# A gated cross-attention and feed-forward block on one core: the layer-normed rows of batches 1 to 3 brought in features first, with means and deviations spread through memory, in place of transpositions on TensorE

## The reference, cut to what matters

```python
x = x + tanh(g_xattn[0]) * xattn(layernorm(x), k_cache=ctx, v_cache=ctx, wq, wk, wv, wo)
x = x + tanh(g_ffn[0])   * ffn(layernorm(x), up, down, up_scale, down_scale, output_scale)

def xattn(x, ...):          # x: (4, 512, 512), ctx: (4, 512, 512)
    q, k_new, v_new = x @ wq.T, x @ wk.T, x @ wv.T
    k, v = concat([ctx, k_new], 1), concat([ctx, v_new], 1)
    return softmax(q @ k.T / sqrt(512)) @ v @ wo.T

def ffn(x, ...):            # hidden 2048, both weights only by their sign
    return relu((x @ sign(up).T) * up_scale) @ sign(down).T * down_scale * output_scale

def layernorm(x):           # no gain and no bias
    return (x - mean(x)) / sqrt(var(x) + 1e-5)
```

## Time and profile before

| What | Value |
|---|---|
| Median of 3 runs | 628.89 us (628.64 to 629.04) |
| The profiled execution's own time | 627.86 us |
| Its span in the trace | 625.8 us |
| Mean granted TensorE clock | 0.999 of full speed |
| PE busy | 617.2 us, 99% of the span |
| DVE, ACT, POOL busy | 247.1, 177.6, 73.9 us |
| Moved by DMA | 30.07 MB, 48 GB/s on average |

### The profile page before, as it was taken

The page is one execution under the profiler, slowest core; times in us unless marked ns, Lnnn a source line. Parts: engine busy times, 40 slices in busy tenths (PEclk is TensorE's granted clock), DMA queues, the critical chain, the costliest instruction groups (busy, mean ns, idle before and its releaser), DMA issues.

```text
span 625.8 us, 6852 instructions
## 1 busy us (share of the span) xinstructions
PE 617.2 (99%) x2898; PEld 513.2 (82%) x2898; DVE 247.1 (39%) x429; ACT 177.6 (28%) x273; POOL 73.9 (12%) x52
## 2 busy tenths in 40 slices
PE   7999999999999999999999999999999999999997
PEld 6888888888888888888888888888888888888885
DVE  4346322226322226222236123543574366436234
ACT  3724221224221224130236243322212221312211
POOL 5750202001202002102002100100010001000002
PEclk9999999999999999999999999999999999999999
DMA  8830201000202000101012323100010010001001
GB/s 299 299 125 1 68 1 67 1 0 1 68 0 68 0 1 0 68 1 68 1 39 96 102 78 125 67 1 0 29 41 0 1 50 18 0 1 68 2 1 67
DMA packets 13518, 30.07 MB, mean 48 GB/s; under 512 B 1456, under 2 KB 1456, under 8 KB 13360
## 3 DMA queue, kind: packets, MB, share of 16 engines
q1 hardware_dynamic: 13488, 29.64, 13.7%
HBM read 25.44 MB, written 4.19 MB: 47 GB/s over the span
## 4 chain that ended last, share of the span: by engine, by line
PE 96%; DVE 2%; ACT 1%; DMA 1%; SPq 0%; issue 0%; ACTq 0%
PE proj L293 32%; PE score L293 21%; PE proj L453 19%; PE score L466 18%; PE turn L285 4%; PE score L396 2%; DMA rows<-in_x 1%; DVE four_x L639 0%; ACT four_x L501 0%; DVE rows L819 0%; DVE raw_ctx L816 0%; DVE neg_max L659 0%; ACT probs L513 0%; ACT probsT L505 0%; ACT weights L522 0%; SPq L172 0%
## 5 line engine op out<-in xcount | busy, mean ns | idle before, releaser
L453 PE MATMUL proj<-four_x,weights 128*128 128x512 f32 x512 | 127.6, 392 | 0.0
L466 PE MATMUL score<-weights,probsT 128*128 128x512 f32 x512 | 126.5, 389 | 0.2 <-DVE probsT L776 0.2
L466 PEld LDWEIGHTS score<-weights,probsT 128*128 128x128 f32 x512 | 96.1, 188 | 20.6 <-DVE probsT L776 0.6
L453 PEld LDWEIGHTS proj<-four_x,weights 128*128 128x128 f32 x512 | 95.2, 188 | 19.4
L293 PE MATMUL score<-four_x 128*128 128x512 f32 x384 | 89.9, 391 | 0.0
L293 PE MATMUL proj<-probsT,four_x 128*128 128x512 f32 x384 | 89.9, 391 | 0.0
L612 ACT ACTIVATE probs<-proj,hid_gain 128x512 f32<-128x512 f32 x64 | 43.9, 687 | 148.0 <-PE proj L453 148.0
L509 ACT ACTIVATE four_x<-proj 128x512 fp32r<-128x512 f32 x60 | 35.8, 599 | 172.6 <-PE proj L293 172.6
L293 PEld LDWEIGHTS proj<-probsT,four_x 128*128 128x128 f32 x384 | 71.5, 188 | 14.6
L293 PEld LDWEIGHTS score<-four_x 128*128 128x128 f32 x384 | 71.5, 188 | 14.6
L645 DVE TENSOR_TENSOR four_x<-proj,four_x 128x512 fp32r<-128x512 f32 x44 | 30.3, 691 | 122.0 <-ACT four_x L509 122.0
(11 more groups left out here) (61 smaller groups left out, 372.7 us busy)
## 6 DMA issues: line engine op xcount, KB each, us to landing
raw_w<-in_ffn_w SPq DMA_DIRECT2D x16, 512.0 KB, 3.3
raw_ctx<-in_ctx_turned SPq DMA_DIRECT2D x4, 1024.0 KB, 5.2
raw_ctx<-in_ctx SPq DMA_DIRECT2D x4, 1024.0 KB, 5.3
result<-rows SPq DMA_DIRECT2D x16, 256.0 KB, 2.0
rows<-in_x SPq DMA_DIRECT2D x3, 1024.0 KB, 6.6
rows<-in_x SPq DMA_DIRECT2D x4, 256.0 KB, 4.5
rows<-in_wk SPq DMA_DIRECT2D x4, 256.0 KB, 6.0
rows<-in_wq SPq DMA_DIRECT2D x1, 1024.0 KB, 8.5
```

Source lines behind the costliest of these rows:

```text
L453: last = pe.matmul(proj[:, j % 2, :], signs[:, j, 0, k * P:(k + 1) * P], four_x[:, c, s, k, :], start=(k == 0 and s == HI), stop=(k == DC ...
L466: last = pe.matmul(wide(r), hid_split[:, j % HR, s, r * P:(r + 1) * P], signs[:, j, 1, :], start=(j == 0 and s == HI), stop=(j == HC - 1 a ...
```

## The change

For batches 1 to 3 the transpositions of the layer-normed rows are gone. The host also hands over x with its last two axes exchanged (`x_turned`, one more input). For each of the three batches:
- SyncE loads batch b's `x_turned` (1 MB) into `turned_x`, which is the buffer of `normed` under a new name;
- VectorE copies the four means of each partition beside the four `rstd` (`means`); SyncE stores those 128 x 8 numbers into a DRAM scratch `row_facts`, waits until that is done, and loads the two lists of 512 back into all 128 partitions (`all_facts`, the buffer of `raw_w`, 512 KB);
- VectorE subtracts the means and multiplies by the deviations, both now along the free axis (`norm_turned`, 128x2048 each); ScalarE copies HI into `xT`, VectorE subtracts for LO (`next_rows_low`);
- VectorE's `norm_rows` and TensorE's `turn_next_rows`, with the evacuations of both, are left to batch 3 alone.

`raw_w` being in use, the first load of feed-forward weights moves from the start to where the others stand, behind all of this.

```diff
+            def next_rows(b):
+                sp.wait_ge(normed_done, RT)
+                if b == 1:
+                    sp.wait_ge(turned, RT)
+                else:
+                    sp.wait_ge(next_lo, b - 1)
+                sp.dma_start(turned_x[:, :, :], x_turned_v[b]).then_inc(turned_x_in, 16)
+                sp.wait_ge(rstd_done, b)
+                sp.wait_ge(means_out, b)
+                sp.dma_start(row_facts[b - 1].rearrange("s r p -> p s r"), mean_rstd[:, :, :],
+                             allow_slow_non_contiguous=True).then_inc(facts_stored, 16)
+                sp.wait_ge(facts_stored, 16 * b)
+                sp.dma_start(all_facts[:, :, :], row_facts[b - 1:b].rearrange("a s r p -> a s (r p)").broadcast_to(
+                    [P, 2, ROWS])).then_inc(facts_in, 16)
+
+            next_rows(1)
             for b in range(1, BATCH):
                 sp.wait_ge(ctx_ready, values_split(b - 1) + 1)
                 sp.dma_start(raw_ctx[:, :, :], ctx_turned_v[b]).then_inc(ctx_in, 16)
                 sp.wait_ge(ctx_ready, turned_split(b) + 1)
                 sp.dma_start(raw_ctx[:, :, :], ctx_v[b]).then_inc(ctx_in, 16)
-
-            for j in range(1, HC):
+                if b + 1 < BATCH:
+                    next_rows(b + 1)
+
+            sp.wait_ge(next_lo, BATCH - 1)
+            for j in range(HC):
                 load_signs(j)
...
@@ GpSimd, inverse_std
+                if 2 <= n <= BATCH:
+                    pool.wait_ge(facts_stored, 16 * (n - 1))
...
@@ TensorE, batch
-                    if e in (1, 2):
+                    if last_batch and e in (1, 2):
                         turn_next_rows(b, 2 * (e - 1))
                         turn_next_rows(b, 2 * (e - 1) + 1)
...
-                    pe.wait_ge(turn_lo, turn0(b) + 3 * RT)
+                    pe.wait_ge(next_lo, b + 1)
...
@@ ScalarE, batch
                     proj_out(m + 4 + e, qT[:, HI, e, :])
-                    if e in (1, 2):
+                    if not last_batch and e == 0:
+                        act.wait_ge(turned_normed, b + 1)
+                        act.activation(xT[:, HI], turned_x[:, :, :], ACT.Copy).then_inc(next_hi, 1)
+                    if last_batch and e in (1, 2):
...
@@ VectorE
+            def norm_turned(b):
+                dve.wait_ge(facts_in, 16 * b)
+                dve.wait_ge(turned_x_in, 16 * b)
+                dve.tensor_tensor(turned_x[:, :, :], turned_x[:, :, :],
+                                  all_facts[:, 0:1, :].broadcast_to([P, DC, ROWS]), ALU.subtract).then_inc(centred, 1)
+                dve.wait_ge(centred, b)
+                dve.tensor_tensor(turned_x[:, :, :], turned_x[:, :, :],
+                                  all_facts[:, 1:2, :].broadcast_to([P, DC, ROWS]), ALU.mult).then_inc(turned_normed, 1)
+            def next_rows_low(b):
+                dve.wait_ge(next_hi, b)
+                dve.tensor_tensor(xT[:, LO], turned_x[:, :, :], xT[:, HI].bitcast(F32), ALU.subtract
+                                  ).then_inc(next_lo, 1)
+            def means(n):
+                dve.wait_ge(meanvar_done, RT * n + RT)
+                if n >= 2:
+                    dve.wait_ge(facts_stored, 16 * (n - 1))
+                dve.tensor_copy(mean_rstd[:, 0, :], mean_var[:, :, 0]).then_inc(means_out, 1)
...
@@ VectorE, batch
                 norm_moments(b + 1)
+                if not last_batch:
+                    means(b + 1)
                 probs_out(b, 1)
-                norm_rows(b + 1, next_tile0)
+                if last_batch:
+                    norm_rows(b + 1, next_tile0)
...
                 proj_out(m + 3, chunk(new_side, 3))
+                if not last_batch:
+                    norm_turned(b + 1)
...
                     proj_out(m + 4 + e, chunk(qT, e))
-                    if e in (1, 2):
+                    if not last_batch and e == 1:
+                        next_rows_low(b + 1)
+                    if last_batch and e in (1, 2):
```

More of the change, by code:

```diff
@@ L14, with gated_block @@
 PASSES = ((HI, HI), (HI, LO), (LO, HI))
-def gated_block(nc, x, ctx_kv, ctx_turned, g_xattn, g_ffn, wk, wq, wv, wo, ffn_w, up_scale, down_scale,
+def gated_block(nc, x, x_turned, ctx_kv, ctx_turned, g_xattn, g_ffn, wk, wq, wv, wo, ffn_w, up_scale, down_scale,
                 output_scale, out):
@@ L31, in gated_block @@
     W_K, W_Q, W_V, W_O = range(4)
-    TURNS_BATCH = 2 * RT + RT
-    TURNS_ALL = RT + TURNS_BATCH * BATCH
+    TURNS_BATCH = 2 * RT
+    TURNS_ALL = RT + TURNS_BATCH * BATCH + RT
     PROJS_FIRST = 2 * DC
@@ L50, in gated_block @@
     ctx_v = ctx_kv.rearrange("b (r p) d -> b p r d", p=P)
+    x_turned_v = x_turned.rearrange("b (c p) k -> b p c k", p=P)
     ctx_turned_v = ctx_turned.rearrange("b (c p) k -> b p c k", p=P)
@@ L73, in gated_block @@
         raw_w = sb("raw_w", [P, 2, DIM])
+        all_facts = raw_w
         normed = sb("normed", [P, RT, DIM])
+        turned_x = normed
         out_gain = sb("out_gain", [P, DIM])
@@ L82, in gated_block @@
         eps = sb("eps", [P, RT])
-        rstd = sb("rstd", [P, RT])
+        mean_rstd = sb("mean_rstd", [P, 2, RT])
+        rstd = mean_rstd[:, 1, :]
+        row_facts = nc.dram_tensor("row_facts", (BATCH - 1, 2, RT, P), F32).ap()
         neg_max = sb("neg_max", [P, RT])
@@ L122, in gated_block @@
         signs_in = sem("signs_in")
+        means_out, facts_stored, facts_in, turned_x_in = map(sem, (
+            "means_out", "facts_stored", "facts_in", "turned_x_in"))
+        centred, turned_normed, next_hi, next_lo = map(sem, ("centred", "turned_normed", "next_hi", "next_lo"))
         ident_zero, ident_ready, half_ready = map(sem, ("ident_zero", "ident_ready", "half_ready"))
@@ L182, in _ @@
             sp.dma_start(hid_gain[:, :], up_scale).then_inc(small_in, 16)
-            load_signs(0)
             sp.wait_ge(w_ready, SPLIT[W_K] + DC)
@@ L335, in turn_next_rows @@
             def turn_next_rows(b, r):
-                pe.wait_ge(normed_done, RT * (b + 1) + r + 1)
+                pe.wait_ge(normed_done, RT + r + 1)
                 turn_job(turn0(b) + 2 * RT + r, cols(normed[:, r, :]))
@@ L470, in turn_next_block @@
             def turn_next_block(c, r):
-                pe.wait_ge(normed_done, RT * (BATCH + c + 1) + r + 1)
+                pe.wait_ge(normed_done, RT * (c + 2) + r + 1)
                 turn_job(TURNS_ALL + RT * c + r, cols(normed[:, r, :]))
@@ L839, in laid_out @@
         'x': given('x'),
+        'x_turned': _np.ascontiguousarray(given('x').transpose(0, 2, 1)),
         'ctx': given('ctx_2048'),
```

## The result

The changed kernel takes 623.43 us (median of 5 runs, 622.95 to 625.68) against 628.64 for the kernel before in the same session: a ratio of 0.9925, interval 0.9906 to 0.9944. The prediction was 623.5 in a range of 622.2 to 625.4. The profiled execution has a span of 620.7 us against 625.8.

What follows compares the result with a forecast made beforehand. TensorE, busy 617.2 of 625.8 us, bounds the kernel. Removing 48 transpositions saves 5.4 us with all additions hidden: 627.86 - 5.4 = 622.5 profiled, plus 1.03 to the median gives 623.5 us, range 622.2 to 625.4.

Steps and rivals of the forecast that it cites:

- The price of a transposition: TensorE's attention stages, batches 0 to 2: 48 transpositions at 0.11 us each, 1.80 us per batch, 5.4 us saved.
- rival 4: A transposition does cost its record, 48 x 0.273 = 13.1 us: 615.8 us; chance 0.01.
- rival 3: TensorE gains nothing in the attention stage because something that ends together with it takes over: 628.9 us; chance 0.03.
- VectorE's additions: Two 2.28 us operations before attention job 0's subtraction, hidden with 3.5 us margin before TensorE's job 2.
- Rival 1: VectorE's operations slower than the slope says; at 4.61 us each, 1.0 us lost a batch: 626.5 us; chance 0.05.
- The facts' way through memory: SyncE's store of 8.5 us and load of 3.3 bring the facts at 66.7, 5.3 us before VectorE asks.
- the cover of 8.8 us: Margin of the allowed 20.8 us over the 12.0 us taken for the facts' store and load.
- Rival 2: Late 4-byte store makes TensorE wait before attention job 2; at 0.30 us per number 635.2 us; chance 0.05.
- the threshold of 20.8: TensorE loses nothing while the facts' store and load together take under 20.8 us, 54.70 to 75.5.
- Costed at nothing: Queues passed, including the first signs' load moved from the start to behind batch 3's context: all at zero.

Runs made afterwards that it cites:

- the experiment: The changed kernel with the 4-byte store of the facts issued twice, the second after the first had landed: 638.77 us, ratio 1.0172.

## Why the prediction was right

**The price of a transposition** was the whole sum, and it held: 1.80 us per batch foretold from distances between starts, 1.82 measured, 5.46 against 5.4. That the 48 cost this and not their records (13.1 us, rival 4) is shown twice, by taking them out alone and by putting them back alone; the stage of 21.76 us, all busy, leaves no room for rival 3. The Trainium skill's figure of about 275 ns per transposition ("TensorE: Matmul & The Clock Gate", Part 4, for bf16) is near this case's record of 273 ns and would have been wrong as a price.

**VectorE's additions** took 2.28 and 2.29 us, foretold as 2.28 by the slope. The margin was 3.9 us, foretold 3.5, and overdrawing it by 0.7 cost 0.8 per batch. Rival 1 was a real mechanism, and its way of pricing held; its condition didn't occur.

**The facts' way through memory** was under-priced: 9.3 to 11.0 us for the store where I took 8.5, 5.3 for the load in two batches and 3.7 in batch 2 where I took 3.3, so about 14.6 for the pair and not 12.0. Two terms were mis-sized: the price per 4-byte piece, 0.102 from a mean over mostly large packets, was about 0.14, and the facts' load was priced like a load of distinct rows. The facts came 2.2 us later than foretold, 68.9 against 66.7, which the cover of 8.8 us swallowed. The Trainium skill's rule that a strided last axis becomes one descriptor per element ("DMA: Bandwidth & Descriptors", Rules for kernel authors) agrees with the trace: packets under 512 bytes rose from 1456 to 4672, by 3216, of which 3 x 1024 = 3072 are these numbers.

**Rival 2's place was right and its price wrong.** In batch 0 of the experiment the pair took 78.80 - 54.4 = 24.4 us and the pause was 3.5, as the threshold of 20.8 has it. But the prediction charged the pause alone. It left out that the granted clock falls behind such a pause, which made the late transfers cost about 60% more than the pauses themselves (16.6 us for 10.2 of pauses). By the prediction's price a pair of 24.7 would give 635.2; the measured kernel, with 24.4 in batch 0, took 638.8. So the harm was understated; the chance isn't tested by one kernel.

**Costed at nothing and not quite nothing:** the feed-forward part was 0.78 us longer, most of it one late start of TensorE, 395.77 us where the eight matmuls before it would have let it start at 395.19. One buffer is loaded, emptied by ScalarE and loaded again sixteen times, and a load of 5.1 us where the others take about 3.2 made TensorE wait for this chain. In order of time, from the late load on:

```profile
362.57 5.11 DMA raw_w<-in_ffn_w
...
367.70 1.07 ACT weights L553
...
390.46 3.51 DMA raw_w<-in_ffn_w
...
394.96 0.68 ACT probs L646
...
395.77 2.08 PE proj L484 x8
```

The kernel before had the same chain close behind: its last Sign began 398.49 - 382.94 = 15.6 us into the feed-forward part, the changed kernel's 393.99 - 377.06 = 16.9, and at 16.1 (the store in larger pieces) TensorE didn't wait yet. So the kernel before had between 0.5 and 1.3 us of cover here. Moving the first load out of the start doesn't by itself use it up: the kernel with the transpositions put back has it moved too, and a feed-forward part of 242.9 us. What the late cases share is the load of instructions; why it falls there isn't settled.

**Luck.** That 623.43 lies within 0.1 us of the forecast is luck. The prediction had 622.5 for the profiled execution and 1.03 from there to the median; measured are 622.95 and 0.48. The start and the feed-forward part, both costed at nothing, moved by 0.41 and 0.78 us in opposite directions. What the runs support is the mechanism and its size, 5.2 us in the medians against 5.4.

## What to carry to other kernels

Price what is taken from a pipelined engine by the distance between starts with and without it, not by its record, and test it by putting idle copies back. Work for other engines is free up to a margin that belongs to one buffer and one moment: find the next job that reads or refills the bank, and count backwards. A wait of a busy TensorE can cost more than its length (here 16.6 us for 10.2 of pauses of 2.6 to 4.1 us), so a transfer put on such a path deserves more margin than its price alone says: here store and load together used 14.6 of the 20.8 us there were. And before a small loss is put down to the change, look at what else went through the DMA engines in that moment, and at a second trace.

## What was not expected of the hardware

After pauses of 2.6 to 4.1 us the granted clock was 0.50 for up to 6 us of the work behind them, after 0.81 us it stayed at 1.00, and filling pauses with small matmuls, wholly or all but 1.6 us, kept it at 1.00. A store of 4 KB from SBUF to memory landed in 1.4 us as 128 pieces of 32 bytes and in 8.3 to 11.0 as 1024 of 4 bytes. The tenth load of 512 KB of weights took 4.5 to 5.4 us in the six traces in which a load of 16 KB of instructions fell into it, and 3.2 to 3.4 in the four in which none did. The load of one list of 4 KB into all 128 partitions took 5.3 us in batches 0 and 1 of the changed kernel and 3.4 to 3.7 where the store before it was short; but in batch 2 it took 3.7 behind the longest store, so the length of the store isn't the reason, and what is stays open.
